# Layer norms of a four-stage block stack: where epsilon is added, and when the mean's sign is turned

## What is computed

```
x = x + attn_block(layernorm(x))   # has two layer norms of its own inside
x = x + rwkv_mix(layernorm(x))
x = x + ssm_scan(layernorm(x))     # state scan over 512 channels x 16 states
x = x + expert_mlp(layernorm(x))
layernorm(x) = (x - mean(x)) / sqrt(var(x) + 1e-5)
```

## Time and profile before

| | |
|---|---|
| runs | 3612.30, 3612.49, 3615.84 us |
| profiled execution | 3620.18 us, its span 3618.1 us |
| TensorE | 84% of the span busy, 17392 matmuls |
| GpSimd | 77%, 2583 instructions |
| VectorE | 71%, 5920 instructions |
| ScalarE | 67%, 5331 instructions |
| mean granted TensorE clock | 0.91 of full speed |

### The profile page before, as it was taken

One profiled execution on the slowest core, in us unless ns is written; L12 is line 12 of the kernel. 1 busy time (PEld: TensorE's weight loads), 2 busy tenths in 40 slices (PEclk: granted clock), 3 DMA queues, 4 the chain that ended last, 5 costly groups with the idle time before them and its releaser, 6 DMA issues.

```text
span 3618.1 us, 58031 instructions
## 1 busy us (share of the span) xinstructions
PE 3042.8 (84%) x17392; PEld 1885.8 (52%) x17392; DVE 2583.2 (71%) x5920; ACT 2415.5 (67%) x5331; POOL 2786.8 (77%) x2583
## 2 busy tenths in 40 slices
PE   5888888897988979899898989889898998987557
PEld 3555454464655646465464646556464654644236
DVE  3356878687787868778686876878687776878870
ACT  4577767676776857677685767768576776855431
POOL 1117989898887979888897988889798888977880
PEclk9998898899999989999898989989898998988678
DMA  2017877877777877877777887778878778789981
GB/s 73 7 42 192 214 208 193 225 215 238 207 204 222 217 229 216 241 209 204 223 218 228 220 237 210 207 222 226 230 215 234 210 204 231 213 248 256 284 235 37
DMA packets 423337, 736.59 MB, mean 204 GB/s; under 512 B 53427, under 2 KB 100147, under 8 KB 423027
## 3 DMA queue, kind: packets, MB, share of 16 engines
q1 hardware_dynamic: 423026, 732.89, 72.3%
HBM read 648.84 MB, written 83.89 MB: 203 GB/s over the span
## 4 chain that ended last, share of the span: by engine, by line
PE 60%; ACT 9%; POOL 9%; DVE 9%; issue 6%; DMA 5%; SPq 2%; ACTq 0%; DVEq 0%; POOLq 0%
PE bank L466 16%; PE bank L474 9%; PE bank L589 6%; PE bank L499 6%; PE bank L736 5%; PE bank L722 5%; PE bank L511 5%; POOL u_rows L1506 4%; PE bank L670 4%; DMA u_rows<-u_dram 3%; PE bank L527 3%; POOL u_rows L1499 3%; DVE u_rows L1287 3%; ACT prob L791 2%; DMA d_rows<-delta_dram 1%
## 5 line engine op out<-in xcount | busy, mean ns | idle before, releaser
L1506 POOL TENSOR_TENSOR u_rows<-u_rows,c_rows 128x512 f32<-128x512 f32 x1024 | 1304.8, 1277 | 169.3 <-DVE state L1292 116.4
L1499 POOL TENSOR_TENSOR u_rows<-u_rows,b_rows 128x512 f32<-128x512 f32 x960 | 1225.8, 1278 | 71.8 <-DMA u_rows<-u_dram 70.8
L962 ACT ACTIVATE bank<-d_rows,a_rep 128x512 f32<-128x512 f32 x1024 | 697.7, 688 | 296.5 <-DMA d_rows<-delta_dram 150.6
L1287 DVE TENSOR_TENSOR_SCAN u_rows<-bank,state,u_rows 128x512 f32<-128x512 f32 x512 | 644.0, 1271 | 83.3 <-ACT bank L962 78.9
L1287 DVE TENSOR_TENSOR_SCAN u_rows<-bank,u_rows 128x512 f32<-128x512 f32 x512 | 622.8, 1216 | 85.0 <-ACT bank L962 81.2
L791 ACT ACTIVATE prob<-prob,neg_max 128x256 f32<-128x256 f32 x1024 | 509.9, 505 | 42.9 <-DVE neg_max L1074 42.7
L670 PE MATMUL bank<-u_rows,sum_n 128*32 128x512 f32 x2048 | 309.1, 679 | 237.9 <-POOL u_rows L1506 235.0
L1074 DVE CUSTOM_DVE_ANT_0 prob<-bank,band 128x256 f32<-128x256 f32 x896 | 337.6, 416 | 178.0 <-PE bank L499 159.8
L511 PE MATMUL bank<-ident,prob 128*128 128x128 f32 x2048 | 330.3, 290 | 89.0 <-ACT prob L791 70.8
L511 PEld LDWEIGHTS bank<-ident,prob 128*128 128x128 f32 x2048 | 247.0, 148 | 230.8 <-issue 185.1
L499 PE MATMUL bank<-kT,q_own 32*128 32x256 f32 x2048 | 299.9, 412 | 47.4 <-DVE neg_max L1074 25.1
(11 more groups left out here) (167 smaller groups left out, 5276.4 us busy)
## 6 DMA issues: line engine op xcount, KB each, us to landing
u_rows<-u_dram SPq DMA_DIRECT2D x1024, 256.0 KB, 5.4
d_rows<-delta_dram SPq DMA_DIRECT2D x1024, 256.0 KB, 5.1
w<-in_W SPq DMA_DIRECT2D x28, 1024.0 KB, 7.2
zs_dram<-region_b SPq DMA_DIRECT2D x64, 256.0 KB, 2.8
xc_dram<-region_b SPq DMA_DIRECT2D x64, 256.0 KB, 2.5
u_dram<-region_b SPq DMA_DIRECT2D x64, 256.0 KB, 3.4
delta_dram<-region_b SPq DMA_DIRECT2D x64, 256.0 KB, 3.1
yg<-xc_dram SPq DMA_DIRECT2D x64, 256.0 KB, 4.9
```

Of the source, the lines that this page charges most:

```text
L962: e.activation(banks[at.bank][:, :], delta_of(i, k), ACT.Exp, scale=a_rep[:, j:j + 1]).then_inc(filled[at.bank], 1)
L1287: e.tensor_tensor_scan(rows, banks[at.bank][:, :], rows, state[:, k:k + 1] if i % 2 else 0.0, ALU.mult, ALU.add).then_inc(drained[at.bank], 1)
L1499: e.tensor_tensor(rows, rows, b_rows[:, :], ALU.mult).then_inc(bx_ready.sem, 1)
L1506: e.tensor_tensor(rows, rows, c_rows[:, :], ALU.mult).then_inc(hc_ready.sem, 1)
```

## The change

GpSimd adds epsilon itself, as soon as the variances are there, and takes the power; VectorE's addition is gone, and its multiplication by -1 no longer stands ahead of the power. GpSimd waits for that product only ahead of its own multiplication of `shift`. The power's semaphore counts three steps a norm where it counted two.

```diff
-                self.power = sem(f"ln_rstd_{name}", 2 * per)
+                self.power = sem(f"ln_rstd_{name}", 3 * per)
...
-            e.wait_ge(*ln.power.at(i, 2 * k + 2))
+            e.wait_ge(*ln.power.at(i, 3 * k + 3))
...
             ins.then_inc(ln.stat.sem, 1)
             e.wait_ge(*ln.stat.at(i, 3 * k + 2))
-            e.tensor_scalar(ln.rstd[:, :], ln.mean_var[:, :, 1], EPS, None, ALU.add)
             e.tensor_scalar(ln.shift[:, :], ln.mean_var[:, :, 0], -1.0, None, ALU.mult).then_inc(ln.stat.sem, 1)
...
         def pool_rstd(e, ln, i, k):
 
+            e.wait_ge(*ln.stat.at(i, 3 * k + 2))
+            e.wait_ge(*ln.out.at(i, k))
+            e.tensor_scalar(ln.rstd[:, :], ln.mean_var[:, :, 1], EPS, None, ALU.add).then_inc(ln.power.sem, 1)
+            e.wait_ge(*ln.power.at(i, 3 * k + 1))
+            e.tensor_tensor(ln.rstd[:, :], ln.rstd[:, :], power[:, :], ALU.pow).then_inc(ln.power.sem, 1)
             e.wait_ge(*ln.stat.at(i, 3 * k + 3))
-            e.tensor_tensor(ln.rstd[:, :], ln.rstd[:, :], power[:, :], ALU.pow).then_inc(ln.power.sem, 1)
-            e.wait_ge(*ln.power.at(i, 2 * k + 1))
+            e.wait_ge(*ln.power.at(i, 3 * k + 2))
             e.tensor_tensor(ln.shift[:, :], ln.shift[:, :], ln.rstd[:, :], ALU.mult).then_inc(ln.power.sem, 1)
```

## The result

Over 22 runs of each, the kernel before took a median of 3615.39 us (3603.22 to 3624.08) and the changed one 3625.40 us (3612.88 to 3633.18). The ratio is 1.0027 [1.0017, 1.0038]: 9.8 us slower, between 6 and 14. The forecast was 4.5 us faster.

A forecast was written before the change was run, and what follows sets the result against it. The prediction took TensorE to set the pace (busy 84%), with the other engines counting where it waits for them. -13.0 us on VectorE and +8.5 on GpSimd made -4.5, from 3612.5 to 3608.0 us, range 3598 to 3626.

The forecast's parts named there:

- VectorE's part: Removing L1044 turns doubled waits for GpSimd single behind rwkv (6.9) and attention (3.7), plus 30 other additions (2.4): 13.0 us gained.
- the scores' wait: TensorE's 1.15 us wait for VectorE ahead of the scores behind rwkv should go, six times: 6.9 us.
- GpSimd's part: Each norm costs GpSimd 0.27 us more, for the addition (0.19) and its gap; 8.5 us lost in all.
- 24 x 0.27: At 24 of 31 powers on the chain GpSimd comes late from scan work, so the full delay counts: 6.5 us.
- 0.06 x 7: At seven powers on the chain GpSimd stands waiting, so the norm comes only 0.06 us later: 0.4 us.
- 6 x 0.27: Three groups' heads lie off the chain within a few tenths of it, counted whole: 1.6 us.
- The copy's line: GpSimd copy times, 0.88 ns an element and 174 ns at four, used as nearest guide to the addition's 190 ns.
- TensorE's idle time ahead of L670: Sign of being wrong: TensorE's wait for GpSimd's scan sums (L1506) grows by over 10 us.
- GpSimd is the bound in more places than one chain shows: Rival: every norm pushes GpSimd's scan back; all 96 delays cost 26 us, less 13.0: 13 us slower, 3625.5; chance 0.18.
- The double wait: Rival of no change: nine places lose a wait and others get one through shifted phase, 3612.5 to 3616; chance 0.07.
- dear: Rival: GpSimd's addition costs what the power does, 1.01 + 0.08 us, 34 us less 13: 3633.5; chance 0.06.
- The "faster" rival: Rival: GpSimd's added time mostly disappears in its waits, costing some 1.5 us against the 13.0 gained: 3601; chance 0.27.

The follow-up runs named there:

- the rest alone: Kernel before with VectorE's epsilon addition (and epsilon) gone in the 64 norms outside the head, nothing added on GpSimd: ratio 0.9968, 12 us faster.
- the sign by columns: Kernel before with VectorE's sign turned by four one-column instructions instead of one, its addition kept: ratio 1.0003, +1 us.
- two spare additions: Kernel before with two unused GpSimd epsilon additions, each waited for, ahead of the power: 35 us slower in all norms, +33 in the head's 32, +1 elsewhere.
- the changed form in the head: Kernel before with the change made only in the head's 32 norms (ln_a, k < 2): ratio 1.0060, 22 us slower.
- with that wait filled: Kernel before with two spare GpSimd additions in the head's norms, plus ten unused identity transposes in TensorE's wait for z: ratio 1.0054, +20 us.
- filling one wait: Kernel before with one VectorE instruction a norm, the head's first norm a step earlier and five matmuls in TensorE's MLP-input wait: ratio 0.9987, -5 us.

## Why the prediction was wrong

**VectorE's part held in size.** The 13.0 us were measured as 9 (4 to 14) over all norms and 12 (5 to 18) in the rest alone. Double waits turned single, the remaining instruction waits as the first one did, and the scores' wait went down 6.6 us, as forecast. That these are the places of the gain is not shown: the sign by columns brought the scores' wait to 5.3 us and no gain, and the kernel with the full gain of 12 still had 7.5.

**The step that failed is GpSimd's part**, "24 x 0.27", "0.06 x 7" and "6 x 0.27", together 8.5 us. The runs show 24 us for GpSimd's side alone, with 0.34 us a norm, and about 22 for the change (10 + 12). Three things were wrong in it:

- *The size of a norm's delay:* 0.40 us, not 0.27. The addition was 0.04 us dearer (227 ns, not 190). I counted a gap for the addition, but none for the second semaphore that the product waits for, 0.065, nor a longer power, 0.023. (The copy's line, 0.88 ns an element, gives 178 ns at four; the 174 named is its value at none. The 190 doesn't hang on it.) Where GpSimd stood waiting, as at the norm of the earlier trace rows, it came 0.14 us later (1.78 us from the aggregation's end to the product's, for 1.64), and not 0.06. By this alone the 32 norms of the heads are 12.8 us, 4 us more than I had for all.
- *What a delay costs in the head:* I took one for one. It cost 1.6 with two spare additions, and 1.7 with the changed form in the head. Behind TensorE's longer waits for z its clock often fell, and with that wait filled the price was one for one. Its share in the whole change, whose profile shows such a fall behind 1 head of 16, isn't settled.
- *What it costs in the rest:* I took those delays as covered. They are, two additions at +1 us, as long as VectorE's waits stand. Without these, one takes back most or all of the gain (-2 for -12). I costed the two sides of the change as if each acted on the kernel before, and added them up.

**The prediction's own marks.** The addition took 0.23 us, just over the 0.22 named; the signs' means and the scores' waits were as said; z came 0.81 us later against the head's first norm, not 0.54. TensorE's idle time ahead of L670 grew by 4.5 us, below the 10 named, and the change was still slower: that mark watched the wrong wait. The one for z, L460, grew by 10.4.

**The rivals.** "GpSimd is the bound in more places than one chain shows" had the direction, at 13 us slower, within the measured 6 to 14. Its mechanism was wrong in place: not many norms evenly, but the 32 of the heads, each for more than its delay. The double wait didn't just move: the sign's means stayed where the addition's had been, and the scores' waits fell. The addition was not dear. The "faster" rival fell with the heads.

The Trainium skill (GPSIMD Engine Reference, "Performance versus the Vector engine") had elementwise work on GpSimd at about twice VectorE's time; the estimate by that page was 0.34 us. The run shows 0.23, 1.35 times VectorE's 0.17 at four elements a row, so here the row was nearer. The rule's warning against the move was right all the same, for reasons that are not in it: the gaps, the second wait and what stands behind the head.

## What to carry to other kernels

An addition moved to another engine isn't an exchange of equal durations: it brings a semaphore gap of its own (83 ns here) and a second wait for the reader that now has two sources (65 ns), together two thirds of the 227 ns that it takes itself. Before such a move, look for the handoff with the tightest chain (here z to TensorE) and ask whether the engine it moves to stands in it; a delay there can also cost clock. And don't add up the two sides of a move from one profile: here a gain on one engine was there only as long as the other wasn't delayed. Where an instruction is to go because it waits, merge it with its neighbour (-8 us here) rather than move it (+10).

## What the hardware showed that I had not expected

- A power of 128x4 on GpSimd takes 1.037 us behind a small GpSimd instruction that it waits for, and 1.01 to 1.02 behind scan work or a wait for VectorE, in every kernel here. The two forms stand side by side where only the rest has the changed one:

```profile
L1393 POOL TENSOR_TENSOR rstd_a<-rstd_a,power 128x4 f32<-128x4 f32 x16 | 16.6, 1037 | 1.3
L1398 POOL TENSOR_TENSOR rstd_a<-rstd_a,power 128x4 f32<-128x4 f32 x32 | 32.3, 1009 | 37.1 <-DVE shift_a L1046 37.1
```

- VectorE's instruction with two SBUF operands waits for GpSimd like the plain one (463 and 647 ns as means), and the one-column instructions show no such wait (141 ns).
- The scatter of the changed kernel's runs, some 20 us, goes with the granted clock, 2.3 us for each 0.001 of its mean. In before's runs the slope is 1.4 to 1.9, and in one kernel of six runs there was none.
- A granted clock raised by filling one wait (0.922 for 0.908 in the profiles, means of the runs 0.923 and 0.910) brought no time that could be measured.
